# Dividing the contexts of three 16-wide attentions by way of device memory instead of by turning them

## The reference

```python
scores = einsum('bihd,bjhd->bhij', q, k) * scale      # causal, 512 x 512
attn   = softmax(scores, axis=-1)                      # exp(s - max) / sum
out    = einsum('bhij,bjhd->bihd', attn, v)
y      = out.reshape(b, s, 512) @ wo
```

## Time and profile before

| what | value |
|---|---|
| median of 3 runs | 1919.49 us (1917.98 to 1922.94) |
| the profiled execution, its own time | 1924.28 us |
| its span, first to last instruction | 1922.6 us |
| busy, share of the span: PE, DVE, ACT, POOL | 95%, 59%, 45%, 45% |
| granted TensorE clock, mean | 0.993 |
| DMA queue 1, share of 16 engines | 15.6% |
| first attention, steps 0 to 15 and end | about 51 to 240 us |
| second (wide) | about 1329 to 1540 us |
| third | about 1633 to 1825 us |

### The profile page before, as it was taken

The page is one execution under the profiler, slowest core; times in us unless marked ns, Lnnn a source line. Parts: engine busy times, 40 slices in busy tenths (PEclk is TensorE's granted clock), DMA queues, the critical chain, the costliest instruction groups (busy, mean ns, idle before and its releaser), DMA issues.

```text
span 1922.6 us, 29645 instructions
## 1 busy us (share of the span) xinstructions
PE 1828.2 (95%) x10760; PEld 1287.9 (67%) x10760; DVE 1130.6 (59%) x2433; ACT 859.2 (45%) x1896; POOL 871.5 (45%) x1383
## 2 busy tenths in 40 slices
PE   7999999999999999999999899999999999999998
PEld 3454447888888888888888687764455454555466
DVE  5677467666666666666666424235556355666465
ACT  1566544444444444444444433314466502565441
POOL 2465426555555555555554444323355312444352
PEclk9899999999999999999999999999999999999999
DMA  7213000101010101010100234205123104211101
GB/s 230 55 46 114 2 18 1 55 1 56 1 55 1 56 1 56 1 56 1 56 1 33 83 115 148 88 1 129 52 69 100 47 1 94 54 36 46 53 10 45
DMA packets 47201, 99.28 MB, mean 52 GB/s; under 512 B 8011, under 2 KB 36043, under 8 KB 43595
## 3 DMA queue, kind: packets, MB, share of 16 engines
q1 hardware_dynamic: 44464, 95.02, 15.6%
q10 hardware_dynamic: 2592, 2.36, 0.5%
HBM read 66.36 MB, written 2.10 MB: 36 GB/s over the span
## 4 chain that ended last, share of the span: by engine, by line
PE 76%; DVE 12%; ACT 4%; issue 3%; DMA 1%; POOL 1%; ACTq 1%; PEld 0%; SPq 0%; PEldq 0%; POOLq 0%; DVEq 0%
PE PS L1483 10%; PE PS L1582 9%; PE PS L485 6%; PE PS L2005 5%; PE PS L595 5%; PE PS L574 4%; PE PS L620 4%; PE PS L1560 4%; PE PS L1544 3%; DVE NM L801 3%; PE PS L2018 3%; PE PS L539 3%; PE PS L1512 3%; PE PS L1976 2%; PE PS L500 2%
## 5 line engine op out<-in xcount | busy, mean ns | idle before, releaser
L1023 ACT ACTIVATE PB<-PS 128x512 f32<-128x512 f32 x480 | 276.4, 600 | 213.1 <-PE PS L574 210.3
L929 POOL TENSOR_SCALAR_AFFINE_SELECT PB<-PB 128x256 f32<-128x256 f32 (+1 forms) x480 | 173.7, 369 | 283.6 <-ACT PB L1023 274.6
L801 DVE TENSOR_REDUCE NM<-PS 128x2 f32<-128x1024 f32 x192 | 206.8, 1090 | 147.3 <-PE PS L541 143.8
L574 PE MATMUL PS<-KQ 99*128 99x512 bf16 (+3 forms) x768 | 179.1, 305 | 9.3 <-ACT PB L1023 4.6
L1774 ACT CAST OTH<-PS 128x512 fp32r<-128x512 f32 x64 | 37.6, 587 | 309.5 <-PE PS L1565 309.5
L1901 POOL TENSOR_SCALAR PR<-PR,RCP 128x512 f32<-128x512 f32 (+3 forms) x256 | 135.5, 540 | 83.3 <-DVE RCP L1704 83.3
L1836 ACT ACTIVATE PR<-PR,NX 128x512 f32<-128x512 f32 (+3 forms) x256 | 145.0, 566 | 32.5 <-DVE NX L1698 29.3
L485 PE MATMUL PS<-XTT,WA 128*128 128x512 f32 x288 | 145.9, 613 | 13.5 <-DVE ident_masks_b L2647 12.0
L1698 DVE CUSTOM_DVE_ANT_0 PR<-PS,CAUSAL 128x512 f32<-128x512 f32 (+3 forms) x256 | 124.3, 486 | 53.3 <-PE PS L1531 52.0
L539 PE MATMUL PS<-KQ 99*128 99x128 bf16 (+2 forms) x576 | 125.2, 278 | 22.6 <-DVE NM L801 20.5
L1662 DVE TENSOR_TENSOR PTL<-PS,PTH 128x384 fp32r<-128x384 f32 (+2 forms) x256 | 115.5, 452 | 28.3 <-ACT PTH L1767 25.9
(11 more groups left out here) (333 smaller groups left out, 4578.4 us busy)
## 6 DMA issues: line engine op xcount, KB each, us to landing
KQ<-HI SPq DMA_DIRECT2D x90, 128.0 KB
KQ<-MID SPq DMA_DIRECT2D x72, 128.0 KB
WB<-f_w SPq DMA_DIRECT2D x12, 768.0 KB, 4.4
WB<-w1o SPq DMA_DIRECT2D x8, 1024.0 KB, 7.9
WC<-f_w SPq DMA_DIRECT2D x10, 768.0 KB, 4.4
WB<-w1a SPq DMA_DIRECT2D x8, 768.0 KB, 4.3
WB<-w1b SPq DMA_DIRECT2D x8, 768.0 KB, 5.8
WA<-w SPq DMA_DIRECT2D x6, 1024.0 KB, 6.4
```

The source lines that it names most:

```text
L574: x = pe.matmul(ps[:, at:at + T - j * P], KQ[0:PR16, self.key(s, h), j * P:(j + 1) * P], KQ[0:PR16, self.query(s, h), j * P:T], start=True ...
L801: x = dve.tensor_reduce(nm[:, h:h + 2, i], PS[:, b:b + 2, 0:(i + 1) * P], AX.X, ALU.max, negate=True)
L929: pool.affine_select(blocks, blocks, [[0, count], [1, P]], ALU.is_ge, 0.0, base=0, channel_multiplier=-1).then_inc(s16["probs_ready"].sem, 1)
L1023: act.activation(PB[:, n % PBS, :], PS[:, 4 + n % 2, :], ACT.Exp, scale=self.scale)\
```

## The change

Groups 0 to 13 (`TURNED` = 14 of them) are no longer turned. SP stores each `OT` into a scratch in device memory (`parts`, 256 KB a group, `keep`). When both groups of a chunk are there, SP loads from it the eight rows of sums, spread over 128 partitions of 32 numbers (`SUMS`, runs of 128 bytes), and the 8 x 16 rows of contexts straight into `XTT` (`collect`). DVE inverts the 128 x 32 sums (`invert`, a = 2 of odd steps from 3); SP stores the inverses to a second scratch (`keep_inverse`) and loads them back with each head's row repeated over its 16 partitions (`SPREAD`, 256 KB, `spread_inverse`); DVE multiplies `XTT` by `SPREAD` in place (`scale_ctx`, a = 2 of even steps from 4, and for the last such chunk, C = 6, at a = 5 of step 15). Groups 14 and 15 are turned and divided as before. `ctx_T` and `take_ctx` are made for the last chunk alone. `pv` of a group waits for the copy of the group before; that of group 15 for `norm` of group 14, which stands behind `scale_ctx` of C = 6 on DVE.

On SP the new transfers stand behind `load_max` and ahead of `load_rows` and `prefetch` of the same pass; `keep_inverse` and `spread_inverse` of C = 6 are in an added pass G = 16, behind the last `prefetch`.

```diff
--- before.py
+++ after.py
@@
-        CTX = sb("CTX", [P, 2, NT, P], F32, A16)
+        CTX = sb("CTX", [P, NT, P], F32, A16)
@@
+        SUMS = sb("SUMS", [P, 32], F32, A16)
+        SPREAD = sb("SPREAD", [P, T], F32, A16)
...
+        parts = nc.dram_tensor("parts", (2, 2 * P, T), F32).ap()
+        inverses = nc.dram_tensor("inverses", (2, 8, T), F32).ap()
...
+        TURNED = NB * GROUPS - 2
         s16 = {k: sig("a16_" + k) for k in (
...
-            "max0_loaded max1_loaded scoresT_ready exp_ready probs_ready pv_ready outT_ready out_psum ctx_ready "
-            "ctxT_psum ctxT_ready biased").split()}
+            "max0_loaded max1_loaded scoresT_ready exp_ready probs_ready pv_ready outT_ready turned_psum normed "
+            "ctxT_ready biased out_kept ctx_loaded inv_loaded").split()}
...
             def __init__(self, W, Wo, nkv, scale, loaded, cols=None, vbias=None, rope=False, bo=None,
@@
-                    outT_ready=16, out_psum=16, ctx_ready=16, ctxT_psum=8, ctxT_ready=8,
+                    outT_ready=16, turned_psum=3, normed=TURNED // 2 + 2, ctxT_ready=8,
+                    out_kept=16 * TURNED, ctx_loaded=16 * TURNED, inv_loaded=16 * TURNED,
@@
-                    pe.wait_ge(on["ctx_ready"].sem, on["ctx_ready"].at(G))
-                    if G % 2 == 0:
-                        pe.wait_ge(on["ctxT_ready"].sem, on["ctxT_ready"].at(G // 2))
+                    pe.wait_ge(on["outT_ready"].sem, on["outT_ready"].at(G))
+                    if G > TURNED:
+                        pe.wait_ge(on["normed"].sem, on["normed"].at(TURNED // 2 + G - TURNED))
@@
-                x.then_inc(s16["out_psum"].sem, 1)
+                x.then_inc(s16["turned_psum"].sem, 1)
...
             def ctx_T(self, pe, C, bank):
...
-                pe.wait_ge(on["ctx_ready"].sem, on["ctx_ready"].at(2 * C + 2))
+                pe.wait_ge(on["normed"].sem, on["normed"].at(TURNED // 2 + 2))
...
-                    x = pe.transpose(PS[:, bank, t * P:(t + 1) * P], CTX[:, C % 2, t, :], ident[:, :])
-                x.then_inc(s16["ctxT_psum"].sem, 1)
+                    x = pe.transpose(PS[:, bank, t * P:(t + 1) * P], CTX[:, t, :], ident[:, :])
+                x.then_inc(s16["turned_psum"].sem, 1)
...
             def out_part(self, pe, b, t, c, bank):
@@
-                        if k == 1 and s >= 3 and s % 2:
-                            self.ctx_T(pe, (s - 3) // 2, 7)
                         if k == 3 and s + 1 < last:
...
                         if k == 3 and s:
...
-                        if k == 8 and s:
+                        if k == 8 and s > TURNED:
@@
             def norm(self, dve, st, G):
...
-                dve.wait_ge(on["out_psum"].sem, on["out_psum"].at(G + 1))
+                dve.wait_ge(on["turned_psum"].sem, on["turned_psum"].at(G + 1 - TURNED))
...
-                if G >= 4 and G % 2 == 0:
-                    dve.wait_ge(on["ctxT_psum"].sem, on["ctxT_psum"].at(G // 2 - 1))
-                c = CTX[:, G // 2 % 2, :, G % 2 * 64:G % 2 * 64 + 64].rearrange("p t (h e) -> p t h e", e=HD)
+                c = CTX[:, :, G % 2 * 64:G % 2 * 64 + 64].rearrange("p t (h e) -> p t h e", e=HD)
...
-                                  ALU.mult).then_inc(s16["ctx_ready"].sem, 1)
+                                  ALU.mult).then_inc(s16["normed"].sem, 1)
+            def invert(self, dve, C):
+                on = self.on
+                dve.wait_ge(on["ctx_loaded"].sem, on["ctx_loaded"].at(32 * (C + 1)))
+                dve.reciprocal(SUMS[:, :], SUMS[:, :]).then_inc(s16["normed"].sem, 1)
+            def scale_ctx(self, dve, C):
+                on = self.on
+                b, c = divmod(C, NC)
+                dve.wait_ge(on["inv_loaded"].sem, on["inv_loaded"].at(32 * (C + 1)))
+                dve.tensor_tensor(XTT[:, b, c, :], XTT[:, b, c, :], SPREAD[:, :], ALU.mult)\
+                   .then_inc(s16["ctxT_ready"].sem, 1)
...
             def vector(self, dve, st):
@@
-                    if s:
+                    if s > TURNED:
@@
+                if a == 2 and s >= 3 and s % 2:
+                    self.invert(dve, (s - 3) // 2)
+                if a == 2 and s >= 4 and s % 2 == 0:
+                    self.scale_ctx(dve, (s - 4) // 2)
+                if a == 5 and s == NB * GROUPS - 1:
+                    self.scale_ctx(dve, TURNED // 2 - 1)
@@
-                act.wait_ge(on["ctxT_psum"].sem, on["ctxT_psum"].at(C + 1))
-                if c == 0:
-                    act.wait_ge(on["proj_psum"].sem, on["proj_psum"].at(self.each * (b + 1)))
-                    act.wait_ge(on["v_psum"].sem, on["v_psum"].at((b + 1) * (NT if self.wide else 1)))
+                act.wait_ge(on["turned_psum"].sem, on["turned_psum"].at(3))
...
             def take_out(self, act, G):
...
+                if 1 <= G <= TURNED:
+                    act.wait_ge(on["out_kept"].sem, on["out_kept"].at(16 * G))
+                elif G > TURNED:
+                    act.wait_ge(on["turned_psum"].sem, on["turned_psum"].at(G - TURNED))
...
             def scalar(self, act):
@@
                 for s in range(last):
                     for k in range(10):
...
-                        if k == 1 and s >= 3 and s % 2:
-                            self.take_ctx(act, (s - 3) // 2, 7)
                         if k == 1 and self.rope and s - 2 in self.late:
...
                         if k == 1 and not self.rope and s - 1 in self.late:
@@
+            def keep(self, sp, G):
+                on = self.on
+                C, e = divmod(G, 2)
+                sp.wait_ge(on["outT_ready"].sem, on["outT_ready"].at(G + 1))
+                sp.dma_start(parts[C % 2, e * P:(e + 1) * P], OT[:, :]).then_inc(s16["out_kept"].sem, 16)
+            def collect(self, sp, C):
+                on = self.on
+                b, c = divmod(C, NC)
+                if c == 0:
+                    sp.wait_ge(on["proj_psum"].sem, on["proj_psum"].at(self.each * (b + 1)))
+                    sp.wait_ge(on["v_psum"].sem, on["v_psum"].at((b + 1) * (NT if self.wide else 1)))
+                sp.wait_ge(on["out_kept"].sem, on["out_kept"].at(32 * (C + 1)))
+                heads = parts[C % 2].rearrange("(h p) n -> h p n", p=32)
+                sp.dma_start(SUMS[:, :], heads[:, HD, :].rearrange("h (p n) -> h p n", n=32))\
+                  .then_inc(s16["ctx_loaded"].sem, 16)
+                sp.dma_start(XTT[:, b, c, :], heads[:, 0:HD, :]).then_inc(s16["ctx_loaded"].sem, 16)
+            def keep_inverse(self, sp, C):
+                on = self.on
+                sp.wait_ge(on["normed"].sem, on["normed"].at(C + 1))
+                sp.dma_start(inverses[C % 2].rearrange("h (p n) -> h p n", n=32), SUMS[:, :])\
+                  .then_inc(s16["inv_loaded"].sem, 16)
+            def spread_inverse(self, sp, C):
+                on = self.on
+                sp.wait_ge(on["inv_loaded"].sem, on["inv_loaded"].at(32 * C + 16))
+                if C:
+                    sp.wait_ge(on["ctxT_ready"].sem, on["ctxT_ready"].at(C))
+                sp.dma_start(SPREAD[:, :], inverses[C % 2].unsqueeze(1).to_broadcast([8, HD, T]))\
+                  .then_inc(s16["inv_loaded"].sem, 16)
             def load_rows(self, sp, m):
@@
-                for G in range(1, NB * GROUPS):
-                    self.load_max(sp, G)
+                for G in range(1, NB * GROUPS + 1):
+                    if G < NB * GROUPS:
+                        self.load_max(sp, G)
+                    if G >= 4 and G % 2 == 0:
+                        self.keep_inverse(sp, (G - 4) // 2)
+                    if 2 <= G <= TURNED + 1:
+                        self.keep(sp, G - 2)
+                        if G % 2:
+                            self.collect(sp, (G - 3) // 2)
+                    if G >= 4 and G % 2 == 0:
+                        self.spread_inverse(sp, (G - 4) // 2)
+                    if G == NB * GROUPS:
+                        break
...
```

## The result

The changed kernel takes 1926.73 us (median of 19 runs), the kernel before 1921.05 beside it (19 runs): ratio 1.0027, 95% interval 1.0019 to 1.0036, so 5 us slower. I had forecast 1.3 us faster; the sign is wrong, and 1926.73 lies inside the range. One of the 19 runs took 3618.73 us at full granted clock, which nothing on record explains, and the ratio leaves it out.

What follows compares the result with a forecast made beforehand. It followed chains of waits through PE, DVE and ACT, with PE busy 95%. Terms -13.6 + 2.1 + 1.9 + 6.6 + 1.7 = -1.3 us on the 1919.5 median gave 1918 us, range 1909 to 1930.

Steps and rivals of the forecast that it cites:

- The 0.44 us of turning: On PE: turning stands in the chain of waits at 31 places, 0.44 us each, 13.6 us less in all.
- The new work in steps 12 and 13: On DVE: multiplication 0.69 and inversion 0.25 us enter the chain beside the layer norm; 2.1 us lost.
- The mechanism at the third end: Third attention's end: inverses queue behind 624 and 1152 KB of weights on one queue; 6.6 us lost.
- rival A: Third attention's end: weights don't hold the inverses up, or not for long; about 1912 us, chance 0.20.
- PE's idle time before `pv` of group 15: At the attentions' ends: about 1.9 us in the first, none in the wide, 6 to 7 in the third.
- that wait hides them: DVE at a = 2: waiting for part 3 of the scores covers inversion (0.25 us) and multiplication (0.69).
- the two hops: Copy to inversion through memory: store 2.4, issue 0.55, load 3.2, sum 6.2 us, so DVE doesn't stall.
- rival D: DVE stalls at `invert` in every odd step; one more us in each gives about 1936 us, chance 0.07.
- In step 14 ... PE turns those rows only at k = 5.: DVE's multiplication waits about 2 us for its transfer in step 14, but PE needs those rows only later.
- The wide attention's end: Chain through memory 13.5 us against 13.88, nothing lost; 512 KB of weights landed before the inverses.
- The terms of the chain: Attention ends, copy to `pv`: stores 2.4 each, loads 3.2 each, plus issue and DVE work; 13.5 us, bounds 10.4 to 16.7.
- Rival C: Attention ends: chain through memory is slower, 16 us or more from copy to `pv`; about 1930 us, chance 0.20.

Runs made afterwards that it cites:

- experiment 5: Changed kernel with DVE's inversion and multiplication at a = 2 moved behind that place's other work; 1923.39 us, ratio 1.0009 to the kernel before.
- Experiment 1: Changed kernel with the last prefetch of weights issued behind the spread inverses instead of ahead of the inverses; 1919.73 us, ratio 0.9990 to the kernel before.
- Experiment 8: Changed kernel with last weights behind the spread inverses, and DVE's inversion and multiplication behind its other work; 1913.06 us, ratio 0.9951 to the kernel before.
- experiment 4: Changed kernel with `load_rows` of the first attention issued ahead of the new transfers; 1930.9 us, ratio 1.0052 to the kernel before.

## Why the prediction was wrong

**Right.** The 0.44 us of turning and the places where it counts: steps with late work are shorter by 0.43 to 0.45 (steps 3 and 6 of the first attention by 0.55 and 0.69, which I can't explain in full), those without, in the third and the wide attention, are unchanged, and leaving out what replaces it gave 14.8 us where the sum had 13.6. The new work in steps 12 and 13: +0.17 net in step 12 (0.60 of 0.69 for the multiplication) and 0.17 of 0.25 for the inversion, as experiment 5 shows by taking both away. The mechanism at the third end, weights ahead of the inverses on one queue, which refutes rival A. PE's idle time before `pv` of group 15: 1.70, 0.44 and 9.01 us, where I had 1.9, none and 6 to 7.

**The step that failed first: "that wait hides them".** I had looked at a = 2 in steps 12 and 13 and found the layer norm there; I hadn't looked at what stands at a = 2 in steps 5, 7 and 9 of the first attention. My 9.6 us from the copy to the next part 3 were right, and the two hops end at 8.0. But 2.2 us of rotation are queued behind the inversion: 8.0 + 0.35 + 2.2 - 9.6 = 0.95, measured 0.80 in step 9. Cost 1.75 us, of which experiment 5 takes back 1.4. I had also written that DVE would have no idle time for a DMA at a = 2 of odd steps. It has some in about half of them, the most in the wide attention, and it costs in 3: rival D in a small form. The question was not whether DVE waits for the transfer, but who stands behind it.

**"In step 14 ... PE turns those rows only at k = 5."** That holds for the layer norm, but another engine is hit. Step 14 is 0.49 longer in the first attention, and experiment 5 takes 0.64 off in the first and the wide one. Timeline of the changed kernel in step 14 of the first attention, and of experiment 5:

```profile
209.12 0.69 DVE L835 TENSOR_TENSOR XTT<-XTT,SPREAD 128x512 f32<-128x512 f32 x1 [2.24 <-DMA SPREAD<-inverses]
209.20 0.67 POOL L935 CAST NM<-NM 128x16 bf16<-128x16 f32 x1
...
210.95 0.23 PE L557 MATMUL PS<-ident_masks_b,NM 128*128 128x128 bf16 x1 [0.54 <-POOL NM L941]
```

```profile
209.89 0.20 POOL L935 CAST NM<-NM 128x16 bf16<-128x16 f32 x1
...
211.15 0.70 DVE L835 TENSOR_TENSOR XTT<-XTT,SPREAD 128x512 f32<-128x512 f32 x1
```

DVE waits 2.24 us for the transfer, so the multiplication comes late and runs beside POOL's work on the maxima of the last group, for which PE waits. Of the 48 instructions of L935 in the trace, this one and the one at the same place of the wide attention take 0.67 and 0.66 us, all others 0.20; the next one (L937), beside the layer norm's L279, takes 0.39 and 0.40 instead of 0.22. Together that is 0.64 us. In experiment 5 none of them is longer than 0.22.

**The third attention's end, the largest miss: mechanism right, size wrong.** 6.6 forecast, 10.0 measured. The term that failed is the weights' landing. I took it from a row in which only the 624 KB ran beside it, 9.5 us; beside the loads of contexts and sums too, issued just ahead, it was 12.6. In the traces without these loads ahead of it, it is 8.3 to 10.6. The load of contexts in turn took 5.0 instead of 3.2, but that cost nothing here, since the inverses waited for the weights. Experiment 1, which changes the order alone, moves this end from 21.59 to 13.49 and the time by 7 us.

**The wide attention's end.** I wrote that the weights had landed before the inverses. They landed at 1508.83 + 5.3 = 1514.1, and the inverses were issued at 1513.57; still these landed after 1.42 us, as with nothing ahead. What the weights lengthened was the load of contexts, issued at 1508.21: 5.0 us to the inversion, 3.9 in the first attention, where nothing runs beside. The chain takes 14.67 where PE alone needs 13.87, so the end lost 0.8. The order alone doesn't give it back: experiment 1 has 4.4 us for the load of contexts, but 4.7 instead of 3.7 for the spreading load, now with the weights behind it, and 14.94 in all. Experiment 8 has 4.0 and 3.9, and 13.90. What lies between these two isn't shown.

**The terms of the chain.** In the first attention it came to 13.16 us where I had 13.5, but by errors that cancel: loads 3.9 and 3.4 instead of 3.2, stores 2.0 and 1.42 instead of 2.4 each. Rival C needed 16 and didn't happen.

Together: 2.1 us in the first attention's steps, 3.4 at the third end, 0.9 at the wide one, less 0.3 at the first: 6.1, the distance between -1.3 and +4.8. That the time lies inside the range is in part luck: the upper part of the range stood for rival C, in which every end comes late, and that isn't what happened. Open stays why the stretches at 1.2 GHz in steps 0 and 1 come in some executions and not in others.

## What to carry to other kernels

When a new instruction that can wait goes into a hand-ordered queue, list what stands behind it in every step where it occurs, not in the steps that one has open; behind the work that is ready anyway, the same wait cost 0.1 us instead of 0.4 to 0.8. A small transfer on which the end of a stage hangs must not be issued behind large ones on its queue, and the landing time of a large one is to be taken with the others beside it. Where a round trip through memory has no work to cover it, at the end of a stage, the old way on the compute engines may be the shorter: with nothing else changed, twelve groups by way of memory and four turned take 0.9972 of the time before, fourteen 1.0027. Once the transfers are issued in a better order and the division stands behind the other work, the two can't be told apart (0.9946 and 0.9951).

## What the runs showed of the hardware

- A 16 KB store that lands in 1.42 us alone landed 8.54 us after its issue behind 1152 KB on the same queue, together with them (7.42 in experiment 4, 8.51 in experiment 5).
- The 256 KB load strided by head took 3.9 to 4.4 us from issue to use with nothing issued behind it (nine ends of attentions in five traces), 5.0 with 512 KB of weights behind it, 5.3 with the loads of `load_rows` behind it, most of them of 128 KB. At the end of the third attention it is 4.97 with the weights behind it and 3.94 without them (experiment 1). Transfers issued later slowed one that was under way.
- In the packet records each of these loads, and those of `SUMS`, has 8 packets of 4 bytes beside its data, each store 16. The records don't name the engines; I take these to be the semaphore's, one for each engine. That agrees with what the Trainium skill says (DMA: Bandwidth & Descriptors, why a DMA increments its semaphore by 16). The 3.2 us that I estimated by it, as for a load of 512 KB on 16 engines, were short: 3.9 alone.
- Small POOL instructions (128 x 16, 0.20 us) took 0.67 and 0.66 beside a DVE multiplication of two operands in SBUF (the changed kernel, step 14 of the first and the wide attention).
- At the ends of the attentions the granted clock fell to 1.2 GHz in or behind PE gaps of 9.01 (changed kernel), 10.59 (experiment 5) and 3.36 us (experiment 8) and behind one of 2.08 (first attention, experiment 8), and stayed at 2.4 behind gaps of 1.71 (experiment 1) and 2.26 (experiment 5, first attention). The length of the gap alone doesn't decide. The gap of 9.01 us cost the 32 matmuls behind it 1.9 us more.
